# Masked keys as reciprocals times a mask and a product of values and mask, in place of penalties on the scores

## The reference, cut to what matters

```python
energy = jnp.einsum('bhqd,bhkd->bhqk', Q, K) / scale
energy = jnp.where(mask == 0, NEG_INF, energy)
attention = jax.nn.softmax(energy, axis=1)
x = jnp.einsum('bhqk,bhkd->bhqd', attention, V)
```

## Time and profile before

| what | value |
|---|---|
| median of three runs | 630.04 us |
| profiled execution: time, span | 629.98 us, 628.1 us |
| PE busy in the span | 525.6 us (84%) |
| DVE busy | 516.3 us (82%) |
| POOL busy | 343.4 us (55%) |
| ACT busy | 307.8 us (49%) |
| granted clock, mean | 0.935 |
| PE penalties L1315, 384 matmuls | 38.5 us busy, 281 ns each |
| POOL normalise L1192, 48 | 172.2 us busy, 3588 ns each |
| DVE maximum L795, 48 | 97.2 us busy, 2025 ns each |

### The profile page before, as it was taken

How to read it: one execution, slowest core, us unless ns; L and a number is a source line. 1 busy time by engine, 2 the same in 40 slices (tenths; PEclk the granted TensorE clock), 3 DMA queues, 4 the chain that set the end, 5 groups by cost and what they waited for, 6 DMA issues and landing times.

```text
span 628.1 us, 14763 instructions
## 1 busy us (share of the span) xinstructions
PE 525.6 (84%) x6137; PEld 359.4 (57%) x6144; DVE 516.3 (82%) x660; ACT 307.8 (49%) x515; POOL 343.4 (55%) x247
## 2 busy tenths in 40 slices
PE   4799999997489999999999999999999664545644
PEld 3677777775366666666666666656665432323322
DVE  4597888888568887887888898888888889999996
ACT  3565676664144464445554464446454442625332
POOL 6401333222316556567758859666857758685540
PEclk9899999999699999999999999999999796778777
DMA  8910000000020011101111011101100000000001
GB/s 199 313 50 2 2 2 3 2 2 2 20 65 11 1 54 55 54 13 45 54 55 41 16 55 54 50 15 47 55 9 9 0 9 8 2 14 18 17 33 36
DMA packets 18629, 23.47 MB, mean 37 GB/s; under 512 B 3013, under 2 KB 16306, under 8 KB 18562
## 3 DMA queue, kind: packets, MB, share of 16 engines
q1 hardware_dynamic: 16642, 21.73, 11.7%
q10 hardware_dynamic: 1920, 0.79, 0.6%
HBM read 18.85 MB, written 1.84 MB: 33 GB/s over the span
## 4 chain that ended last, share of the span: by engine, by line
PE 30%; DVE 23%; POOL 14%; issue 5%; ACT 1%; DVEq 0%; POOLq 0%; ACTq 0%
DVE negmax L795 8%; POOL work L1192 8%; PE scores L1328 5%; PE head_out L1357 5%; PE scores L1338 5%; PE wide L1423 4%; PE scores L1315 3%; PE wide L1412 3%; DVE den L803 2%; DVE work L901 1%; PE small L1434 1%; DVE work L897 1%; DVE unit L888 1%; DVE rden L808 1%; DVE x_r L860 1%
## 5 line engine op out<-in xcount | busy, mean ns | idle before, releaser
L1192 POOL TENSOR_TENSOR work<-work,rden 125x1792 f32<-125x1792 f32 x48 | 172.2, 3588 | 106.1 <-DVE rden L808 106.1
L1038 ACT ACTIVATE work<-scores 125x896 f32<-125x896 f32 x96 | 88.2, 976 | 106.4 <-PE scores L1338 104.9
L795 DVE TENSOR_REDUCE negmax<-scores 125x112 bf16<-125x1792 f32 x48 | 97.2, 2025 | 36.4 <-PE scores L1328 36.4
L803 DVE TENSOR_REDUCE den<-work 125x56 f32<-125x896 f32 x96 | 102.8, 1071 | 13.7 <-ACT work L1038 12.7
L1338 PE MATMUL scores<-negmax,identb 125*125 125x448 bf16 x192 | 47.2, 369 | 10.4 <-DVE negmax L795 8.8
L1357 PE MATMUL head_out<-work,v 125*32 125x112 f32 x1536 | 52.2, 268 | 3.0 <-POOL work L1192 2.9
L316 DVE TENSOR_REDUCE a_mpad<-a_s_ps 112x8 bf16<-112x896 f32 x32 | 33.5, 1092 | 22.0 <-PE a_s_ps L490 18.9
L1328 PE MATMUL scores<-qz,kT 32*125 32x224 f32 x768 | 49.8, 373 | 0.0
L1477 PE MATMUL wide<-identb,qv 128*128 128x128 bf16 x112 | 13.5, 296 | 43.2 <-POOL qv L1249 35.7
L1357 PEld LDWEIGHTS head_out<-work,v 125*32 125x32 f32 x1536 | 36.4, 109 | 22.2 <-issue 12.4
L1412 PE MATMUL wide<-ctxT,ck 128*128 128x375 f32 x128 | 48.6, 502 | 0.0
(11 more groups left out here) (214 smaller groups left out, 1119.2 us busy)
## 6 DMA issues: line engine op xcount, KB each, us to landing
ctx_sb<-in_ctx SPq DMA_DIRECT2D x16, 375.0 KB
mask_sb<-in_mask_Bx1xSxS_if SPq DMA_DIRECT2D x32, 164.1 KB
xsx<-in_x SPq DMA_DIRECT2D x4, 448.0 KB, 9.2
out_x<-ores SPq DMA_DIRECT2D x6, 256.0 KB, 2.1
a_raw_w<-in_L_ffn_gate_w SPq DMA_DIRECT2D x1, 1024.0 KB, 5.9
a_raw_w<-in_L_ffn_up_w SPq DMA_DIRECT2D x1, 1024.0 KB, 8.4
a_raw_w<-in_L_ffn_down_w SPq DMA_DIRECT2D x1, 1024.0 KB, 10.4
xt<-xsx SPq DMA_DIRECT2D x4, 112.0 KB, 2.2
```

The lines of the kernel that those rows point to most:

```text
L795: dve.tensor_reduce(negmax[0:KP, :], scores[0:KP, :, 0:4 * TOK].rearrange("p j (h t) -> p t j h", h=4), AX.XY, ALU.max, negate=True).then_ ...
L803: link(dve.tensor_reduce(den[0:KP, kc, half], ex2[0:KP, kc, :, half, :].rearrange("p g t s -> p t g s"), AX.XY, ALU.add))
L1038: act.activation(ex2[0:KP, kc, 4 * i:4 * i + 4].rearrange("p (j m) t s -> p j m s t", m=NE), scores[0:KP, 2 * i:2 * i + 2, 0:4 * TOK].rear ...
L1192: pool.tensor_tensor(ex2[0:KP, kc], ex2[0:KP, kc], over, ALU.mult).then_inc(s["prob"], 1)
```

## The change

The scores get no penalties. The 16 heads of a masked key thus have ordinary weights after the exponential; they are made zero by multiplying the reciprocal `rden` by `stays` (1 where the key stays, 0 where it is masked), a new POOL instruction ahead of each `normalise`, with a wait for its own result. The share that a masked key gives, V/16, is a product of its own on PE, `masked(q, kc)`: `flat` (the values of a chunk, 125 keys x 256) times `even` (1/16 where masked, else 0), two f32 matmuls of 112 columns a chunk, which also start the accumulation in `head_out`.

For these, DVE makes `gone` (1/16 or 0, bf16, 112 tokens on the partitions) from a mask that is now loaded once; PE transposes it (`mask_T`, three bf16 transposes into the upper part of the bank `head_out`); ACT reads the result twice, as `even` and as `stays` (`masks`), and copies the values once more without gaps (`flat_values`, 125 x 768 f32).

In PE's order all penalties go. less_max(now,0) moves ahead of the head outputs of (old,1), whose two calls now stand together behind value 2. `masked` stands ahead of each pair of head-output calls, `mask_T(new)` ahead of key(new,0,0). In step 0, `weight_T(2)` also waits for `gone_read` 2.

```diff
         def load_mask(sp, b, r):
-            halves = mask[b, 0].rearrange("(u t) k -> t u k", u=2)
-            for n in range(2):
-                sp.dma_start(mask_sb[64 * n:64 * n + HALF, r], halves).then_inc(in_mask[r], 16)
+            sp.dma_start(mask_sb[:, r], mask[b, 0]).then_inc(in_mask[r], 16)
...
         ctxT = sb("ctxT", [P, 2, NE, KEYS])
-        pen = sb("pen", [P, 2, 2, NKC, KP], BF16)
+        gone = sb("gone", [TOK, NKC, KP], BF16)
+        even, stays = sb("even", [KP, 2, NKC, TOK]), sb("stays", [KP, 2, NKC, TOK])
+        flat = sb("flat", [KP, 2, NKC, D])
+        plus_one = sb("plus_one", [KP, 1])
...
+        gone_T = head_out[0:KP, D:].bitcast(BF16)[:, 0:NKC * TOK]
         def scale_parts(p):
...
-                def penalty(q):
+                def masked_out(q):
                     b, r, half = q
-                    wait(dve, in_mask[r], 32 * half + 32)
-                    wait(dve, s["s_ps"], 3 * b - 3)
-                    dve.tensor_scalar(pen[:, r], mask_sb[:, r].rearrange("t u (p c) -> t u c p", c=NKC), 0, PEN,
-                                      ALU.is_equal, ALU.mult).then_inc(s["pen"], 1)
+                    wait(dve, in_mask[r], 16 * half + 16)
+                    wait(dve, s["gone_ps"], b)
+                    dve.tensor_scalar(gone[:], mask_sb[:, r].rearrange("t (p c) -> t c p", c=NKC), 0, 1.0 / H,
+                                      ALU.is_equal, ALU.mult).then_inc(s["gone"], 1)
...
+                def flat_values(q):
+                    b, r, _ = q
+                    wait(act, s["wide_read"], values_read(b))
+                    act.copy(flat[:, r].rearrange("p k (n s d) -> p (k n) s d", s=2, d=DH),
+                             v[0:KP, r, :, :, 0:3:2, :].rearrange("p k n s d -> p (k n) s d")).then_inc(s["flat"], 1)
                 def queries(q):
...
                     wait(act, s["pv"], 3 * b + 3)
+                    wait(act, s["gone_ps"], min(b + 3, B))
                     wait(act, s["y_ps"], b - 1)
                     act.copy(oT[:, r].rearrange("p g t -> p (g t)"), head_out[:, 0:NE * TOK]).then_inc(s["oT"], 1)
+                def masks(q):
+                    b, r, _ = q
+                    wait(act, s["gone_ps"], b + 1)
+                    act.copy(even[:, r].rearrange("p c t -> p (c t)"), gone_T)
+                    act.activation(stays[:, r].rearrange("p c t -> p (c t)"), gone_T, ACT.Identity, bias=plus_one[:, 0:1],
+                                   scale=-float(H)).then_inc(s["gone_read"], 1)
...
                     wait(pool, s["rden"], 3 * b + kc + 1)
+                    wait(pool, s["gone_read"], b + 1)
+                    link(pool.tensor_tensor(rden[0:KP, kc, :], rden[0:KP, kc, :], stays[:, r, kc], ALU.mult))
                     over = rden[0:KP, kc, :].unsqueeze(1).unsqueeze(3).to_broadcast([KP, NPAIR, TOK, 2])
...
-                def penalties(q, kc, i):
-
-                    b, r, _ = q
-                    wait(pe, s["exp"], 6 * b + 2 * kc - 1 + i)
-                    for u in range(2):
-                        for n in range(2):
-                            bank = scores[0:KP, 2 * i + n, 0:4 * TOK].rearrange("p (a t) -> p a t", t=TOK)
-                            pe.matmul(bank[:, :, u * HALF:(u + 1) * HALF], pen[64 * n:64 * n + HALF, r, u, kc, :],
-                                      identb[64 * n:64 * n + HALF, 64 * n:64 * n + HALF].unsqueeze(1).to_broadcast([HALF, 4, HALF]),
-                                      start=(u == 0), stop=False, skip_group_check=True)
-
                 def score(q, kc):
                     b, r, _ = q
-                    penalties(q, kc, 1)
+                    wait(pe, s["exp"], 6 * b + 2 * kc)
                     for m in range(NE):
                                              qz[rows, r, m].rearrange("p s t -> p (s t)"),
-                                             start=False, stop=False, skip_group_check=True)
+                                             start=(m == 0), stop=False, skip_group_check=True)
                     last.then_inc(s["s_ps"], 1)
...
+                def masked(q, kc):
+                    b, r, _ = q
+                    if kc == 0:
+                        wait(pe, s["flat"], b + 1)
+                        wait(pe, s["oT"], b)
+                        wait(pe, s["gone_read"], min(b + 2, B))
+                        if b == 0:
+                            pe.wait_ge(s["w_sb"], 3)
+                    for c in range(NE):
+                        pe.matmul(head_out[:, c * TOK:(c + 1) * TOK],
+                                  flat[:, r, kc, c * P:(c + 1) * P],
+                                  even[:, r, kc], start=(kc == 0 and c == 0), stop=False, skip_group_check=True)
                 def head_outputs(q, kc, chunk):
                         wait(pe, s["prob"], 3 * b + kc + 1)
-                        wait(pe, s["wide_read"], values_read(b))
-                        if kc == 0:
-                            wait(pe, s["oT"], b)
-                            if b == 0:
-                                pe.wait_ge(s["w_sb"], 3)
                     for n in range(2):
                             last = pe.matmul(pair_output(h), pair_values(KP, r, kc, h), ex2[0:KP, kc, j % 2 * 4 + j // 2 * 2 + chunk, :, n],
-                                             start=(kc == 0 and chunk == 0 and n == 0),
-                                             stop=(kc == NKC - 1 and n == 1), skip_group_check=True)
+                                             start=False, stop=(kc == NKC - 1 and n == 1), skip_group_check=True)
                     if chunk == NE - 1:
                         last.then_inc(s["pv"], 1)
+                def mask_T(q):
+                    b, r, _ = q
+                    wait(pe, s["gone"], b + 1)
+                    if b == 1:
+                        pe.wait_ge(s["w_sb"], 2)
+                    for kc in range(NKC):
+                        last = pe.transpose(gone_T[:, kc * TOK:(kc + 1) * TOK], gone[:, kc], identb[0:TOK, 0:TOK])
+                    last.then_inc(s["gone_ps"], 1)
...
                         pe.wait_ge(s["w_sb"], 2)
+                        pe.wait_ge(s["gone_read"], 2)
                     if i >= 3:
...
                         pe.wait_ge(s["w_sb"], 1)
-                        pe.wait_ge(s["pen"], 1)
                         pe.wait_ge(s["bv_parts"], 1)
-                        penalties(now, 0, 0)
                     if now:
                         value(now, 1)
-                    if old:
-                        head_outputs(old, 1, 0)
-                    if now:
                         less_max(now, 0)
                         weight_T(1)
-                    if now:
-                        penalties(now, 1, 0)
                     if old:
+                        masked(old, 1)
+                        head_outputs(old, 1, 0)
                         head_outputs(old, 1, 1)
...
                     if old:
+                        masked(old, 2)
                         head_outputs(old, 2, 0)
                         head_outputs(old, 2, 1)
-                    if now:
-                        penalties(now, 2, 0)
                     if new:
+                        mask_T(new)
                         key(new, 0, 0)
...
                         less_max(now, 2)
+                        masked(now, 0)
                         head_outputs(now, 0, 0)
                         head_outputs(now, 0, 1)
-                    if now and new:
-                        wait(pe, s["pen"], n + 2)
-                        penalties(new, 0, 0)
                     if n == B - 1:
```

More of the change, by code:

```diff
@@ L24 @@
 NEG_SELF = -1.0e9
-PEN = -(2.0 ** 100)
 EPS = 1e-5
@@ L1149, in _ @@
                     if new:
+                        masks(new)
                         keys(new, 0)
```

14 lines of the change are left out of this document (8 added, 6 removed).

## The result

The changed kernel takes 633.18 us, the median of 20 runs (630.28 to 634.91), against 630.04 for 20 runs of the kernel before on the same chip (627.98 to 633.46). In a second series the ratio came to 1.0033 (1.0010 to 1.0055). It is slower by a little more than can be told from no change. The forecast was 627.0 with a range of 622 to 632.5: the sign is wrong, and the median lies just outside the range. The profiled execution took 634.35, span 632.3.

What follows compares the result with a forecast made beforehand. The prediction took PE's order of work as the bound, busy 261.6 of 274 us in cross-attention. Its terms, -0.2 +1.0 -1.0 -4.3 +0.1 +0.4 -0.25 +1.2, sum to -3.05 us: 629.98 to 627.0, range 622 to 632.5.

Steps and rivals of the forecast that it cites:

- the term +1.0: Batch 0: weight_T(2) waits for ACT's masks, score +1.5 us later; about 0.5 back without penalties, so +1.0 us.
- less_max waits for the maximum at 3.26: In each part of a batch, PE's less_max can start 3.26 us after the score's start, once DVE's maximum is there.
- Penalties out, ordinary batches: Ten ordinary batches: PE loses penalty groups and gains products and mask transposes; 0.43 us less each, -4.3 us together.
- A, B and C: Parts of a batch, score to score: chunk 0 to 1, 1 to 2, 2 to next batch; forecast 6.50, 6.56, 6.58 us.
- rival 2: Gain eaten by PE change-over (product 0.48 to 0.55) or POOL's multiply at 0.7: 628.8 to 632 us, chance 0.24.
- Rival 3: PE's product weights not loaded ahead: 0.107 us more a record, 646 us, or 632 to 636 in part; chance 0.13.
- POOL's multiply: Ahead of each normalise on POOL: 0.45 us with its link, 48 of them 22 us, slack enough in ordinary batches.
- ACT's readings, flat values and masks: On ACT: flat_values 0.78 us and two mask readings about 0.95, costing nothing, with 0.1 to 0.3 us of cover.
- Batches 8 and 10: POOL does extra work between normalises; PE waits 1.0 us for it, batch 20.7 for 20.66: +0.1 us for both.
- Batch 15: The last batch ends like batch 8 but has no mask_T and key: -0.25 us.
- Batch 12: DVE is the limit there, through a POOL result that comes 0.67 us later: +0.4 us.
- Batch 1, the start and the end: Batch 1 loses its PE wait, -1.0 us; the block's start -0.2; the end, slow product and FFN behind it, +1.2.

Runs made afterwards that it cites:

- experiment 4: Changed kernel with PE's matmuls of flat values times mask left out, their waits kept: 623.74 us, ratio 0.9893 to the kernel before.
- experiment 5: Kernel before with all penalty matmuls left out and nothing in their place: 611.68 us, ratio 0.9708 to the kernel before.
- experiment 2: Changed kernel without POOL's multiply of the reciprocals by stays and its link: 625.49 us, ratio 0.9913 to the kernel before.
- experiment 3: Changed kernel with the multiply by stays moved from POOL to DVE, behind the reciprocal: 629.2 us, ratio 0.9965 to the kernel before.
- experiment 7: Changed kernel with weight_T(2) behind the last keys and DVE's rounding behind chunk 1's second sum and reciprocal: 623.31 us, ratio 0.9883 to the kernel before.
- experiment 10: experiment 7's kernel with POOL's deviation of the next tokens moved ahead of chunk 1's normalise: 634.67 us, ratio 1.0050 to the kernel before.
- experiment 9: Kernel before with only DVE's rounding moved behind the sum and reciprocal of chunk 1: 642.79 us, ratio 1.0184 to the kernel before.
- experiment 6: Changed kernel with chunk 1's head outputs in halves at their old places, product with the first half: 634.03 us, ratio 1.0058 to the kernel before.
- experiment 8: experiment 7's kernel with the multiply by stays on DVE behind the reciprocal instead of on POOL: 638.22 us, ratio 1.0131 to the kernel before.
- experiment 1: Changed kernel with weight_T(2) in step 0 moved behind the last keys, its wait kept: 628.67 us, ratio 0.9966 to the kernel before.

## Why the prediction was wrong

Two steps failed. In batch 0 the term +1.0 has the new wait right but lets PE go on behind it as before, and PE came back at half speed. In batches 8, 10 and 15 "less_max waits for the maximum at 3.26" was taken from an undisturbed batch, and DVE's time was not summed anew where DVE rounds beside POOL's normalise. By its own steps:

- **Penalties out, ordinary batches: right in time.** -4.38 for -4.3, with A, B and C to 0.05. Experiments 4 and 5 confirm the two sides of it. Two sizes were off against each other, and that the sum came out is in part luck. The product's slot was 0.52, not 0.44, which was named as a sign of being wrong (over 0.5) and belongs to rival 2. It was made good because less_max lost 0.09 of its slot. The trace of before had a row for this that was not used: less_max ahead of value 2 has a slot of 0.81 (483.66 to 484.47), against 0.90 ahead of the head outputs. There is also a slip in adding up: the forecast parts, 6.50, 6.56 and 6.58, make 19.64, which is 0.46 under 20.10 and not 0.43.
- **Rival 3, weights in the open: not seen.** Its full price was 0.22 a record, and the product took 0.13. A small part of it could be in the 0.08 that the slot is over the forecast; no run separates that from rival 2's change-over.
- **POOL's multiply: right**, 0.50 to the start of normalise for 0.45 (331.62 to 332.12).
- **ACT's readings, flat values and masks: right**, nothing in ordinary batches (0.82, 0.45, 0.58).
- **DVE's mask: the same 0.66 for 375 elements a partition as for 750** before; hidden, so it costs nothing either way.
- **Batch 0: mechanism of the wait right, the term +1.0 wrong by 2.8 us.** From the batch's first score, the score of chunk 2 was forecast to start 14.4 us on (189.85 - 175.49) and started 14.46 on (191.82 - 177.36), with 12.89 before. Here too two errors met: the readings ended 0.4 earlier than forecast, and the slow weight piece took 0.4 more. Behind it the forecast let PE go on as before. It went on at 0.50 of its clock for some 6 us: 0.4, 0.8 and 1.7 in the three groups, 2.9 together. In the three executions with batch 0 at 21.6 the miss is 1.4.
- **Batches 8 and 10: +1.33 for +0.1.** The step that failed is "less_max waits for the maximum at 3.26": it was read from an undisturbed batch and put unchanged into the batches where DVE rounds. There DVE's load was not summed. POOL's wait was right in place, 0.69 for 1.0. The mechanism (POOL 0.5 later, x_r held until it is done, maximum 1 us late) is shown by experiments 2, 3 and 7: x_r took 0.84, 1.16 and 1.79 as normalise ended 0.3, 0.6 and 1.2 us after its start (experiments 2 and 3, the changed kernel).
- **Batch 15: +1.09 for -0.25**, by the late maximum (A 7.47 as in 8 and 10), the wait of 0.68 for POOL, and 0.7 for slow head outputs behind it (1.72 for 1.01). All three are gone in experiments 2 and 7.
- **Batch 12: +0.70 for +0.4.** DVE was named as the limit, and a POOL result 0.67 later as the cause; less_max waits 1.22 and 1.56 for DVE there. Without POOL's multiply (number 2) the batch is 1.15 shorter, and with the deviation brought forward (number 10) B is 6.53 again, so POOL's results do set DVE's time; only the size was off.
- **Batch 1, the start and the end: right** to 0.3, the start only if the slow stretch at 11 us is taken out.

The error in the profiled execution, 5.1 us in the sum once the 2.1 at the start are taken out, is 2.8 of batch 0, 1.2 of 8 and 10, 1.3 of 15, 0.3 of 12, and small terms of the other sign. The rivals held neither of the two causes: all four were about PE's product and POOL's multiply in themselves, none about what a later POOL does to DVE or about PE's clock behind the new wait.

## What to carry to other kernels

Work out the special batches with the same care as the ordinary one: here ten of sixteen came out to 0.1 us, and the sign was decided in the others, 0, 8, 10, 12 and 15. When an operation of POOL moves by half a microsecond, look at what DVE runs in that stretch, and sum DVE anew. A new wait that leaves PE idle for 2 us or more has to be priced twice, once as it is and once with the matmuls behind it at half speed, since here either could follow; if the waiting group can go behind others, put it there first. The same move of DVE's rounding gained 5 us in one kernel here and lost 12 in another, so such a move has to be tried again whenever either engine's times change.

## What the runs showed of the hardware

**DVE operations held by a POOL operation.** DVE's two operations of the rounding (a scalar_tensor_tensor with two inputs in SBUF, and an in-place clip in bf16), where they started while POOL's 3.59 us tensor_tensor ran, ended just after it in every such place of the thirteen profiles: the first 0.53 to 0.56 us after (0.62 once, where its own length was the limit), up to 1.79 long for 0.63; the clip 0.14 to 0.16 after, 3.55 to 3.56 long for 0.29 to 0.91 elsewhere. Reductions and reciprocals beside the same POOL operation took their usual 1.03 to 1.08 and 0.85. A scalar_tensor_tensor of DVE with one of its inputs in PSUM (`unit`) took its usual 1.2 to 1.3 beside it and could end 2.1 us before it (503.60 before, 1.28 long, in a normalise from 503.40 to 507.00). The Trainium skill ("SBUF — State Buffer", Who interferes with whom) says that a DVE instruction with two SBUF inputs, or one in a 2-port mode, contends with a GpSimd (POOL) instruction that reads SBUF for a port pair that is an exclusive lock, and that the one issued first blocks the other. The traces agree in who waits and for how long. They add that the holder isn't always untouched: normalise took 3.90 to 3.97 for 3.59 in the three kernels where the clip came during it, and its usual 3.58 to 3.59 where x_r did; no run tells why.

**The clock after an idle time.** In the profiled execution PE's granted clock was 1.00 from 178 to 188 us. After 2.75 us of idle it was 0.50 from 191 to 197; in three others of the six executions with this wait the keys behind it took 2.81 to 2.83 instead of 3.87. The waits of 1 us and more in batches 0 to 14 of the thirteen profiles, and the groups behind them:

| PE's wait, us | groups behind it |
|---|---|
| 1.0 to 1.7 | all at their usual times |
| 1.83 and 1.84 (number 9, batches 8 and 10) | slow (values 1.91 and 1.82 for 1.03) |
| 1.99 (number 4, batch 12) | slow (head outputs 1.72 for 1.00) |
| 2.25, 2.26 and 2.60 (batch 12 of numbers 6, 5 and 9) | slow |
| 2.75 (batch 0, six executions) | slow |
| 3.05 (number 8, batch 8) | usual |
| 3.04, 3.42 and 4.71 (numbers 8, 10 and 8) | slow |

The length of the wait alone doesn't decide: 3.05 and 3.04 in one execution differ, and in batch 15 the same 1.89 has the next two groups slow in some executions and not in others.

**Slots depend on the neighbour.** A group of four 125x448 bf16 records has a slot of 0.90 ahead of the 32-column head outputs and 0.81 ahead of the product, whose stationary operand has 128 columns, or of the values' group (125 columns, 483.66 to 484.47 before).

**Still open:** what brings the slow stretch at 11 us in some executions. The stage's granted clock is printed 1.00 for 11 to 16 us in either kernel, so the trace doesn't name it there, and no experiment went into it. In experiment 1 the same kind of stretch came at 18 us instead (eight records in 2.05), and there the granted clock is 0.53 for 18 to 25 us.
